# A graph network's fourth layer: its sums turned by transposing DMA transfers instead of TensorE transposes, each projected two tiles behind

## The reference

```python
h = jnp.maximum(_layernorm(x, axis=-1), 0.0)
x = x + _L3_gnn_ref(h, adj, L3_gnn_t, L3_gnn_weight)

def _L3_gnn_ref(x, adj, t, weight):
    ts = t[0]
    support = x @ weight
    return (1.0 - ts) * support + ts * (adj @ support)
```

## Time and profile before

| | |
|---|---|
| Median of 3 runs | 964.7 us (964.52 to 965.52) |
| Profiled execution | 965.67 us |
| Its span | 964.0 us |
| Fourth layer's sums begin (at full supply) | about 788 us |
| Last sums end | about 952 us |
| TensorE, VectorE, ScalarE busy over the span | 933.9, 743.3, 540.9 us |

### The profile page before, as it was taken

One profiled execution on the slowest core, in us unless ns is written; L12 is line 12 of the kernel. 1 busy time (PEld: TensorE's weight loads), 2 busy tenths in 40 slices (PEclk: granted clock), 3 DMA queues, 4 the chain that ended last, 5 costly groups with the idle time before them and its releaser, 6 DMA issues.

```text
span 964.0 us, 18964 instructions
## 1 busy us (share of the span) xinstructions
PE 933.9 (97%) x7105; PEld 689.2 (71%) x7105; DVE 743.3 (77%) x1112; ACT 540.9 (56%) x934; POOL 94.1 (10%) x206
## 2 busy tenths in 40 slices
PE   9889999999999999999999999999999989999995
PEld 8457788888888888888888455555788845555553
DVE  7697899999999999999996776656447755655664
ACT  6476899999999999999985611111223331111010
POOL 4100001000010001000030000000024430000000
PEclk9899999999999999999999999999999999999998
DMA  4915276677576666658312425655247726666642
GB/s 178 96 45 77 23 100 76 66 89 96 48 96 83 81 66 86 86 51 109 46 39 100 173 94 203 211 183 203 114 181 281 276 79 213 215 227 205 201 153 65
DMA packets 39883, 120.80 MB, mean 125 GB/s; under 512 B 4604, under 2 KB 24597, under 8 KB 39701
## 3 DMA queue, kind: packets, MB, share of 16 engines
q1 hardware_dynamic: 27653, 97.94, 29.0%
q0 software_dynamic: 10944, 21.30, 25.5%
q10 hardware_dynamic: 1232, 0.85, 0.3%
HBM read 169.48 MB, written 14.50 MB: 191 GB/s over the span
## 4 chain that ended last, share of the span: by engine, by line
PE 84%; DVE 7%; ACT 3%; issue 2%; POOL 2%; DMA 0%; POOLq 0%; DVEq 0%; ACTq 0%
PE f_ya L1318 23%; PE f_yb L1318 23%; PE f_ya L1495 14%; PE f_ya L1433 12%; DVE f_gb L1856 2%; PE f_ya L1269 2%; PE f_yb L1404 2%; PE f_yb L1376 2%; PE f_yb L1269 1%; PE f_ya L1442 1%; POOL f_gv L960 1%; ACT f_ubuf L1184 1%; ACT f_x_mat L1186 1%; DVE f_stats L1600 1%; PE f_yb L1302 1%
## 5 line engine op out<-in xcount | busy, mean ns | idle before, releaser
L1318 PE MATMUL f_ya<-f_x_mat,f_s_mat 128*128 128x257 f16 x2028 | 334.6, 273 | 1.9 <-DVE f_x_mat L1664 1.9
L1318 PE MATMUL f_yb<-f_x_mat,f_s_mat 128*128 128x257 f16 x2028 | 333.2, 273 | 0.0
L1318 PEld LDWEIGHTS f_yb<-f_x_mat,f_s_mat 128*128 128x128 f16 x2028 | 198.2, 98 | 24.8
L1318 PEld LDWEIGHTS f_ya<-f_x_mat,f_s_mat 128*128 128x128 f16 x2028 | 194.5, 98 | 27.2 <-issue 2.8
L1030 ACT ACTIVATE f_gb<-f_e_tile,f_expc 128x256 f32<-128x256 f32 x338 | 144.5, 494 | 9.3 <-DVE f_s_mat L1694 9.3
L1856 DVE SCALAR_TENSOR_TENSOR f_gb<-f_gb 128x1664 f32<-128x1664 f32 x52 | 97.7, 1886 | 18.0 <-DMA f_gb<-adj_dram 18.0
L1689 DVE SCALAR_TENSOR_TENSOR f_s_mat<-f_wm,f_s_mat 128x1792 f16<-128x1792 f32 (+1 forms) x52 | 98.4, 1892 | 12.1 <-ACT f_s_mat L1041 8.5
L1683 DVE TENSOR_TENSOR f_wm<-f_gb,f_a 128x1792 f32<-128x1792 f32 (+1 forms) x52 | 98.1, 1887 | 3.2 <-issue 1.6
L1684 DVE SCALAR_TENSOR_TENSOR f_gb<-f_gb,f_a 128x1792 f32<-128x1792 f32 (+1 forms) x52 | 98.1, 1887 | 0.0
L1694 DVE SCALAR_TENSOR_TENSOR f_s_mat<-f_gb,f_s_mat 128x1792 f16<-128x1792 f32 (+1 forms) x52 | 98.0, 1886 | 0.0
L1041 ACT ACTIVATE f_s_mat<-f_wm 128x1792 f16<-128x1792 f32 (+1 forms) x52 | 82.5, 1587 | 22.0 <-DVE f_wm L1683 20.9
(11 more groups left out here) (185 smaller groups left out, 938.2 us busy)
## 6 DMA issues: line engine op xcount, KB each, us to landing
f_gb<-adj_dram SPq DMA_DIRECT2D x52, 832.0 KB, 5.0
f_a<-f_a_dram SPq DMA_DIRECT2D x23, 832.0 KB, 5.9
f_wm<-f_a_dram SPq DMA_DIRECT2D x16, 832.0 KB, 4.6
f_rows<-adj_dram POOLq DMA_DIRECT2D x24, 416.0 KB, 8.2
f_a<-adj_t_dram POOLq DMA_DIRECT2D x26, 224.0 KB, 4.9
f_a_dram<-f_a SPq DMA_DIRECT2D x26, 224.0 KB, 5.3
f_a<-adj_t_dram POOLq DMA_DIRECT2D x26, 192.0 KB, 6.9
f_a_dram<-f_a SPq DMA_DIRECT2D x26, 192.0 KB, 4.2
```

Source lines behind the costliest of these rows:

```text
L1318: return pe.matmul(bank[:, 0:F + 1], s_mat[:, j, side, i], x_mat[:, j, x_side, 0:F + 1], start=start, stop=stop)
```

## The change

For tiles 2 to 23 TensorE no longer turns z. ScalarE copies z from SBUF to fp16 (`high_part`), VectorE takes the low half from SBUF as well (`low3`), and ScalarE issues four DMA transfers that transpose 128 x 128 fp16 each (32 KB), from `z16` to `z16_t`, both in SBUF: two for the high half once it is copied, two for the low half once VectorE signals it. Both are double, for even and odd tiles. ScalarE waits ahead of the copy for the transfers of tile t - 2 (`z16_here`) and for its projection. TensorE projects tile t - 2 at place 20 of tile t, after a wait for `z16_here`. Tiles 0, 1, 24 and 25 are turned on TensorE as before; 24 and 25 are projected from there too.

The order of the engines changes with it. On VectorE the low half of t now stands right behind z of t, and then comes the update of t - 2. In tile 3 TensorE turns tile 1 at place 3 and projects it at place 10; in tile 25 it turns tile 24 at 13, projects tile 23 at 20 and tile 24 at 24. The rest of the program is the same. The core of the diff:

```diff
+                def high_part(t, p, n, reuse=True):
+
+                    a.wait_ge(z_done[3], t + 1)
+                    if reuse:
+                        a.wait_ge(z16_here[p], 64 * n)
+                        a.wait_ge(p_done[3], t - 1)
+                    a.activation(z16[:, p, 0, :], y_sb[:, p, 0:F], ACT.Copy, scale=Z3).then_inc(zt_hi, 1)
+                    a.wait_ge(zt_hi, t + 1)
+                    settle()
+                    for half in range(2):
+                        if half == 1:
+                            a.wait_ge(zt_done[3], t + 1)
+                            settle()
+                        for c in range(FB):
+                            a.dma_start(z16_t[:, p, half, c, :], z16[:, p, half, c * P:(c + 1) * P], transpose=True)\
+                             .then_inc(z16_here[p], 16)
...
+                with a.Fori(0, PAIRS // 2 - 1) as k:
                     for i in range(2):
-                        pair(2 * k + 1 + i, i)
-                turned_copy(TILES - 1)
+                        for p in range(2):
+                            t = 4 * k + 4 + 2 * i + p
+                            product(t, p, 1 - i)
+                            high_part(t, p, 2 * k + 1 + i)
...
-                        pe.wait_ge(zt_done[3], t + 1)
+                        if on_chip:
+                            pe.wait_ge(zt_done[3], t + 1)
+                        else:
+                            pe.wait_ge(z16_here[p], 32 * (t - p))
+                            settle()
...
-                LATE_AT = ({13: (2, 0, False), 20: (2, 1, True)},
-                           {3: (2, 0, False), 8: (2, 1, False), 15: (1, 0, False), 22: (1, 1, False)})
-                STEADY_AT = {EPILOGUE_AT[3][i]: (1, i, False) for i in range(2)}
+                START_AT = ({13: (2, 0, False), 20: (2, 1, True)}, {3: (2, 0, False), 10: (2, 1, False)})
+                STEADY_AT = {20: (2, 1, False)}
+                END_AT = {13: (1, 0, False), 20: (2, 1, False), 24: (1, 1, False)}
...
+                        product(0, 0, 1)
+                        product(1, 1, 1)
+                        low3(0, 0)
+                        low3(1, 1)
+                        for t in range(2, 4):
+                            product(t, t % 2, 0)
+                            low3(t, t % 2)
+                            update(t - 2, t % 2, 0, True)
+                            check(CHECKS1 + 2 + t, 1 - t % 2)
```

More of the change, by code:

```diff
@@ L699, in fast_program @@
         extra_here = [sem(f"extra_here{b}") for b in range(2)]
+        z16_here = [sem(f"z16_here{b}") for b in range(2)]
         slot_here = [sem(f"slot_here{b}") for b in range(4)]
@@ L1194, in turned_copy @@
                 def turned_copy(t):
-                    a.wait_ge(zt_psum[3], t + 1)
+                    a.wait_ge(zt_psum[3], t + 1 if t < 2 else t - TILES + 5)
                     a.activation(zt16[:, 0], ep[:, 0:F], ACT.Copy, scale=Z3).then_inc(zt_hi, 1)
-                def pair(k, s, first=False):
-                    for p in range(2):
-                        t = 2 * k + p
-                        if not (first and p == 0):
-                            turned_copy(t - 1)
-                        if first and p == 0:
-                            product(0, 0, s)
-                            product(1, 1, s)
-                        if not first:
-                            product(t, p, s)
@@ L1215, in _ @@
+                for t in range(TILES - 2, TILES):
+                    product(t, t % 2, 1)
+                    turned_copy(t)
             @block.tensor
@@ L1533, in _ @@
                             tile3(8 * k + 2 + 2 * i + p, (1 + i) % 4, i % 2, p, 16 * k + (32 if i == 3 else 16), STEADY_AT)
+                for t in range(TILES - 8, TILES):
+                    q, p = t // 2, t % 2
+                    tile3(t, q % 4, 1 - q % 2, p, 16 * (q // 4) + 16, END_AT if t == TILES - 1 else STEADY_AT)
                 layer_epilogue(3, TILES - 1, 1, 0)
@@ L1996, in _ @@
                     else:
-                        pair(0, True, r=1)
-                        with v.Fori(0, (PAIRS - 2) // 2) as k:
-                            for i in range(2):
-                                pair(2 * k + 1 + i, False, r=i)
-                        pair(PAIRS - 2, False, r=0)
-                        pair(PAIRS - 1, False, True, r=1)
+                        product(0, 0, 1)
+                        product(1, 1, 1)
+                        low3(0, 0)
[5 more added lines that the diff above has]
+                            check(CHECKS1 + 2 + t, 1 - t % 2)
+                        with v.Fori(0, (PAIRS - 3) // 2) as k:
+                            for i in range(2):
+                                for p in range(2):
+                                    t = 4 * k + 4 + 2 * i + p
+                                    product(t, p, 1 - i)
+                                    low3(t, p)
+                                    update(t - 2, p, 2 * k + 1 + i)
+                                    check(CHECKS1 + 2 + t, 1 - p)
+                        t = TILES - 2
+                        product(t, 0, 1)
+                        low3(t, 0)
+                        update(t - 2, 0, PAIRS - 2)
+                        check(CHECKS1 + 2 + t, 1)
+                        v.wait_ge(check_done, CHECKS)
+                        v.tensor_reduce(flags[:, 0:1], bad[:], AX.X, ALU.add).then_inc(flc, 1)
+                        v.wait_ge(flc, 9)
+                        v.tensor_reduce(flags[:, 8:9], flags[:, 0:8], AX.X, ALU.add).then_inc(flagd, 1)
+                        update(t - 1, 1, PAIRS - 2)
+                        product(t + 1, 1, 1)
+                        update(t, 0, PAIRS - 1)
+                        low3(t + 1, 1)
                     if layer == 2:
```

28 lines of the change are left out of this document (20 added, 8 removed).

## The result

The changed kernel takes **1007.9 us** (median of 4 runs, 1005.7 to 1009.1) against 965.1 for the kernel before (4 runs, 964.5 to 965.5): a ratio of 1.0441, 95% interval 1.0422 to 1.0460. The forecast was 963.7 us, with a range from 961.0 to 970.0. The loss is 43 us; "ScalarE is held by its issues", the rival (c), was the third in likelihood, and it is what happened.

A forecast was written before the change was run, and what follows sets the result against it. The prediction took TensorE to bound the kernel. Transposes saved (-4.8 us) and new waits at the layer's beginning (+2.5) and end (+1.3) summed to -1.0, so 964.7 became 963.7 us, range 961.0 to 970.0.

The forecast's parts named there:

- rival (c): Steady tiles: DMA issues hold ScalarE, deciding from 0.92 us each; 971 us at 1.0, 988 at 1.2; chance 0.16.
- What bounded the kernel before: Fourth layer: TensorE's work sets the time, 6.49 us per tile with no wait of TensorE, 6.27 without its transposes.
- What goes: Steady tiles: two TensorE transposes of 0.22 us together leave each of 22 tiles, saving 4.8 us on TensorE's path.
- ScalarE's ring: Steady tiles, z to next z: 2.6 us plus four issues; at 0.81 us each 5.8 us, under 6.27, costing nothing.
- (d): Steady tiles: transfers land late, deciding from 5.4 us; 970 us at 6 us landing, 994 at 8.2; chance 0.11.
- The far end of the bracket: Steady tiles: a transposing issue at twice the plain 0.81 us, 1.62 us, would give a tile of 9.1 us.
- Landing: Steady tiles: the 32 KB transfers land in under 5 us, with 5.5 us available, so TensorE does not wait.
- The beginning of the layer: Tile 3: TensorE's projection of tile 1 waits 2.6 us for VectorE's update of tile 0; net cost 2.5 us.
- The end: Tile 25: TensorE's projection of tile 24 waits 1.3 us for VectorE's update of tile 23.
- Rival (a): Tile 3: the clock falls to half speed for 3.5 to 6 us, costing 1.7 to 3 us: 965.4 to 966.7; chance 0.18.
- Rival (b): Layer's two ends: the new waits are smaller than computed; 959.8 us with neither, 961.1 with only the end's; chance 0.10.
- The sum: Whole kernel: -4.8 + 2.5 + 1.3 = -1.0 us, from a median of 964.7 to 963.7 us; forecast's chance 0.45.

## Why the prediction was wrong, point by point

**What bounded the kernel before: right.** A steady tile without its transposes is 6.27 us when nobody holds TensorE; the layer shows 52.00 of 52.00 us in the runs with none, one, two and plain transfers.

**What goes, 4.8 us: right.** With both new waits taken away the kernel is 4.3 us faster than before, 2.9 at the same clock and with 1.6 us more outside the span (below); the sum says 4.8.

**ScalarE's ring: wrong, and this is the step that failed.** It failed in two terms. The first is the issue. I took 0.81 us from a plain issue as "the nearest on the dear side"; it was plain, and a transposing one is another instruction, 1.27 us at the median. Plain ones in this very place took 0.57. The second is the rest of the ring, which I put at 2.6 us and which took 3.2. From the rows of the turn: L1897 starts 0.68 us after L1194, not 0.50, and L1194 starts 0.46 after the last issue ended, not at once. I had summed an engine's times and left out what lies between a DMA issue and the next ACTIVATE. With 3.2 the ring fits into 6.27 only up to an issue of (6.27 - 3.2) / 4 = 0.77 us. So my own 0.81 would already have made the tile 6.44, or 4 us more in all. "Costs nothing" stood on a margin of 0.11 us per issue, between a borrowed price and a bound that was itself 0.15 too high.

**Rival (c): right in mechanism, too cheap.** I had priced it at 1.0 and 1.2 us, 971 and 988 us, and given it 0.16. At the measured 1.27 my formula gives 2.6 + 5.1 = 7.7 us per tile; it was 8.3, by the 0.6 of the rest and, for a little, the slow issue in every fourth tile. The sign that I had named for (c), TensorE idle at the start of a tile, did not come: it waited at place 20, 19.2 us for transfers and 13.1 for the update, which was my sign for (d). Only the chain, with no TensorE in it, tells the two apart. The far end of the bracket that I had named, 1.62 us and 9.1 us per tile, contained it, and I let neither the forecast nor the range be moved by it. VectorE: DVE Perf Modes of the Trainium skill, "The three transpose paths", lists 1309 ns for a 128 x 128 bf16 transpose by the crossbar DMA. I had weighed it as four transfers in a row, 5.2 us, and as a hold of ScalarE, 998 us. The trace agrees with the second reading, at 1.27 us per issue, though one issue of four blocks took 1.25 as well.

**Landing, rival (d): right that it costs nothing here, wrong in size.** I took "under 5 us and no wait". The median was 2.8 us, but in ten of the 22 tiles the last transfer landed 5.2 to 7.0 us after its issue began, and these are the ten that TensorE waited for, 19.2 us in all. The one ahead of the wait of 3.00 us that is shown at the end was issued at 823.6:

```profile
L1211 ACTq DMA_TRANSPOSE f_s_mat<-f_s_mat x1: 1401/1401/1401, 823.6 to 823.6; - x1
DMA to landing us min/median/max: 6.5/6.5/6.5
```

It cost nothing only because ScalarE's ring was longer still. With two transfers a last one landed up to 5.7 us after its issue, and always at least 1.7 us before its use; with four and the scale ahead the landing was the limit.

**The beginning of the layer: right.** 2.30 us against 2.6, in the projection of tile 1 and released by the update of tile 0. **The end: right.** 1.18 against 1.3. Taking away the first gave 2.5 us (965.6 to 963.1).

**Rival (a), the clock: wrong for tile 3.** Its 3.5 to 6 us at half speed had only rows 10 behind them, still 0.50 some 6 us after the wait; none gives the 3.5. The granted clock stayed at 1.00 in the 4 us behind that wait:

```profile
804.00:808.00 4.00, 4.00 (x23) 2.06 (x22) 1.86 (x2) 0.00 (x0) 0.00 (x0) 1.00 0.24 62
```

**Rival (b), smaller waits:** 2.30 and 1.18 against 2.6 and 1.3, no more than that.

**The sum.** For a kernel that fits its issues into the tile the sum said 963.7. Four such kernels gave 964.9, 965.6, 965.8 and 965.1, with ratios between 0.9997 and 1.0009, where the sum is 0.9990. The interval of one of them leaves 0.9990 out. In the span the gain is there. The median spans of the four are 961.5, 962.0, 962.5 and 961.8 us, against 963.0, 963.0, 962.7 and 963.0 for the kernel before beside them: 1.0 less on average, as the sum says. The layer shows it too, from its first sums to its last projection: 164.4 us with two transfers (786.27 to 950.64) against 167.2 before, of which 1.7 is the slower start of its first 41 matmuls. What took the gain back lies outside the span. I had carried over the 1.67 us between the span and the time (964.0 and 965.67) as if it were fixed. It was 1.6 to 2.0 us in 70 executions of the kernel before and 3.0 to 3.8 in all of the changed ones, those without any transposing transfer too. It comes with the changed program, and why is open.

## What to carry to other kernels

A DMA issue is an instruction of the engine that issues it, and it counts in any ring that goes through that engine, although the profile's busy share doesn't show it. Price it from an issue of the same kind, or, where no row has one, from a bracket whose dear end is allowed to move the forecast, and add what lies between the issue and the engine's next work. Look at when the last transfer of a group lands, not at the median. Then prefer few large transfers to many small ones, and an engine whose next instruction nobody waits for: here halving the count alone took a loss of 4.4% to none, and with the two new waits taken out the idea is worth 0.3 to 0.4%.
